# Last graph layer of a GNN kernel: where TensorE makes the relu inputs and the messages, relative to its table picks

## Reference

```python
h = relu(x @ pre_w1 + pre_b1) @ pre_w2 + pre_b2          # 16 -> 256 -> 256
msg = relu(h[src] @ conv_w + conv_b)                     # one row of 256 per edge
agg = segment_sum(msg, dst, num_segments=h.shape[0])
h = concatenate([h, agg], axis=-1)
out = tanh(relu(h @ post_w1 + post_b1) @ post_w2 + post_b2)
```

## Time and profile before

| | |
|---|---|
| median of 3 runs | 23847.17 us (23841.38 to 23860.08) |
| profiled execution | time 23829.4 us, span 23827.7 us |
| PE, matmuls | 19018.8 us busy, 80% of the span |
| DVE | 13388.2 us, 56% |
| POOL | 17485.7 us, 73% |
| ACT | 2359.5 us, 10% |
| `message_sums` | about 20054 to 23420 us of the span |

### The profile page before, as it was taken

The page is one execution under the profiler, slowest core; times in us unless marked ns, Lnnn a source line. Parts: engine busy times, 40 slices in busy tenths (PEclk is TensorE's granted clock), DMA queues, the critical chain, the costliest instruction groups (busy, mean ns, idle before and its releaser), DMA issues. The chain is left out here.

```text
span 23827.7 us, 301790 instructions
## 1 busy us (share of the span) xinstructions
PE 19018.8 (80%) x104646; PEld 12073.6 (51%) x104646; DVE 13388.2 (56%) x24950; ACT 2359.5 (10%) x5692; POOL 17485.7 (73%) x15117
## 2 busy tenths in 40 slices
PE   0688871787873488888888888499999988999997
PEld 0344431344442355555555555277777765555556
DVE  2688882454543366555555566355555543666662
ACT  0000000000000011111111111011111111111111
POOL 5777775777775788888888887588888853777775
PEclk9888885888886688888888888689999988999998
DMA  2222221111111112221111111133333313777773
GB/s 95 50 60 61 61 58 20 39 44 39 44 39 26 25 31 35 38 33 31 31 31 31 31 31 28 42 52 49 49 52 49 50 24 123 231 229 230 231 231 115
DMA packets 1967855, 1652.07 MB, mean 69 GB/s; under 512 B 781607, under 2 KB 1735622, under 8 KB 1949334
## 3 DMA queue, kind: packets, MB, share of 16 engines
q0 software_dynamic: 892288, 467.38, 14.2%
q10 hardware_dynamic: 821300, 579.22, 7.8%
q1 hardware_dynamic: 252898, 587.74, 7.3%
HBM read 949.01 MB, written 684.18 MB: 69 GB/s over the span
## 5 line engine op out<-in xcount | busy, mean ns | idle before, releaser
L1347 PE MATMUL node_sums<-placed_row,lane_values 128*128 128x392 bf16 x34500 | 6168.6, 338 | 524.6 <-DVE placed_row L1335 524.5
L1405 POOL DMA_INDIRECT acc<-column_sums,sum_rows x3375 | 5683.0, 1684 | 1192.8 <-issue 1139.8
L803 POOL DMA_INDIRECT gathered<-gat_table,src_index x4906 | 4853.9, 989 | 1525.2 <-issue 1500.3
L1347 PEld LDWEIGHTS node_sums<-placed_row,lane_values 128*128 128x128 bf16 x34500 | 3456.9, 102 | 2953.9 <-DVE placed_row L1335 548.7
L1626 POOL DMA_INDIRECT gathered<-sheaf_table,src_index x3125 | 3391.1, 1085 | 959.1 <-issue 946.5
L2408 POOL DMA_INDIRECT gathered<-message_table,src_index x2381 | 2428.6, 1020 | 907.9 <-issue 700.7
L1335 DVE TENSOR_SCALAR placed_row<-iota_rows_f,src_row 128x1568 bf16<-128x1568 f16 x2875 | 1794.5, 649 | 1116.3 <-PE node_sums L1347 1087.1
L1010 PE MATMUL lanes_ps<-S,table_parts 128*128 128x512 bf16 x8892 | 2075.7, 396 | 288.4 <-DVE S L875 288.4
L1010 PE MATMUL lanes_ps<-code_onehot,table_parts 128*128 128x512 bf16 x8892 | 2071.3, 396 | 276.1 <-DVE code_onehot L875 275.9
L1010 PEld LDWEIGHTS lanes_ps<-S,table_parts 128*128 128x128 bf16 x8892 | 896.0, 102 | 1411.0 <-DVE S L875 272.6
L2500 PE MATMUL lanes_ps<-code_onehot,table_parts 128*128 128x384 bf16 x9672 | 1597.9, 327 | 10.2 <-DVE code_onehot L2434 10.2
(11 more groups left out here) (478 smaller groups left out, 22582.7 us busy)
## 6 DMA issues: line engine op xcount, KB each, us to landing
message_rows<-gathered ACTq DMA_DIRECT2D x250, 1600.0 KB, 10.5
src_rows<-src_rows SPq DMA_DIRECT2D x200, 640.0 KB
src_rows<-src_rows SPq DMA_DIRECT2D x125, 960.0 KB
code_rows<-src_code_rows SPq DMA_DIRECT2D x336, 256.0 KB, 3.3
gat_rows<-scanned ACTq DMA_DIRECT2D x25, 3375.0 KB
gathered<-gat_table,src_index POOLq DMA_INDIRECT x4906
acc<-column_sums,sum_rows POOLq DMA_INDIRECT x3375
gat_rows<-scanned ACTq DMA_DIRECT2D x25, 2125.0 KB, 6.9
```

What stands on the lines that cost most here:

```text
L803: g.indirect_dma_start(G[b][:, j, :], None, tab, bass.IndirectOffsetOnAxis(ap=IX[b][:, j:j + 1], axis=0)).then_inc(s_g[b], 16)
L1347: last = pe.matmul(o.acc[:, m, 0:Q8 // 4], lane, o.OW[r][:, m * (Q8 // 4):(m + 1) * (Q8 // 4)], start=first(k, 1) and i == 0 and part == 0 ...
L1405: g.indirect_dma_start(self.acc[i], bass.IndirectOffsetOnAxis(ap=o.IXS[b][:, j:j + 1], axis=0), o.SV[b][:, j, :], None, compute_op=ALU.add ...
```

## The change

PE's steps for a set are written in another order, and ACT's with them. `hidden` (step 4) and `messages` (step 6) are now functions with a half as an argument. PE makes the relu inputs of half 0 after the first 21 of half 1's 39 picks (`FIRST` is 7, and 7 codes by 3 parts are 21). It makes the messages of half 1 after the first 21 picks of half 0 of the next set. The messages of half 0 and then the relu inputs of half 1 follow the picks. ACT copies half 1 of the set before at the start of its turn, and then does relus 0, copy 0, relus 1 and the DMAs. What is computed, and in how many instructions, stays the same; DVE's, POOL's and SP's programs are untouched in this function.

```diff
+                    def hidden(k, h):
+                        pe.wait_ge(s_mk, k * 2 + (h + 1))
+                        if not first(k, 1) or h == 1:
+                            pe.wait_ge(s_re, k * 2 + h)
+                        for m in range(2):
+                            last = pe.matmul(hp[m][:, 0:HE], W1R[:, m * P:(m + 1) * P], MK[h][:], start=True, stop=True)
+                        last.then_inc(s_hid, 1)
+
+                    def messages(k, h):
+                        pe.wait_ge(s_re, k * 2 + (h + 1))
+                        if not first(k, 1):
+                            pe.wait_ge(s_ev, k * 2 + (h - 1))
+                        for j in range(HB):
+                            to = op[h][j // 2][:, j % 2 * HID:(j % 2 + 1) * HID]
+                            for m in range(2):
+                                pe.matmul(to, HS[h][:, m, j * P:(j + 1) * P], WC[:, m, :], start=m == 0, stop=False)
+                            last = pe.matmul(to, ones[:], brow[:], start=False, stop=True)
+                        last.then_inc(s_out, 1)
+
                     def pick(k, b):
                         for h in range(2):
                             if not first(k, 1):
                                 pe.wait_ge(s_mk, k * 2 + (h - 1))
                             for t_ in range(CODES):
                                 if h == 0 and t_ in (0, FIRST):
+                                    if t_ and not first(k, 1):
+                                        messages(k - 1, 1)
                                     pe.wait_ge(s_og, k * 2 + (1 if t_ == 0 else 2))
+                                if h == 1 and t_ == FIRST:
+                                    hidden(k, 0)
                                 for i in range(PARTS):
...
-                        for h in range(2):
-                            pe.wait_ge(s_mk, k * 2 + (h + 1))
...
-                            last.then_inc(s_out, 1)
+                        messages(k, 0)
+                        hidden(k, 1)
                     chunks(pe, count - 1, peel, pick, RING)
+                    messages(count - 2, 1)
...
+                        if not first(k, 1):
+                            copy(k - 1, b, 1)
                         if not last_k(k):
-                            for h in range(2):
...
+                            relu(0)
+                            if not first(k, RING - 1):
+                                a.wait_ge(s_o[nb], 32 * ((k + 1) // RING) if isinstance(k, int) else k * 8 + (8 - 8 * nb))
+                            elif k == RING - 2:
+                                a.wait_ge(s_tb, 1)
+                            copy(k, nb, 0)
+                            relu(1)
                         a.wait_ge(s_done, k + 1)
```

More of the change, by code:

```diff
@@ L2533, in store @@
                         nb = (b + 1) % RING
-                        if not last_k(k):
[L2535 to L2551, removed]
@@ new lines, in relu, with copy @@
+                        def relu(h):
+                            a.wait_ge(s_hid, k * 2 + (h + 1))
+                            if not first(k, 1):
+                                a.wait_ge(s_out, k * 2 + (h - 1))
+                            for m in range(2):
+                                ins = nc.scalar.activation(HS[h][:, m, :], hp[m][:, 0:HE], ACT.Relu, bias=b1["pre_b1"][:, m:m + 1])
+                            ins.then_inc(s_re, 1)
+                        def copy(n, to, h):
+                            a.wait_ge(s_out, n * 2 + (h + 1))
+                            col = PC + h * HB
+                            nc.scalar.activation(G[to][:, col:col + 2, :], op[h][0][:].rearrange("p (a f) -> p a f", f=HID), ACT.Relu)
+                            nc.scalar.activation(G[to][:, col + 2, :], op[h][1][:, 0:HID], ACT.Relu).then_inc(s_ev, 1)
@@ new lines, in store @@
+                        if not first(k, 1):
+                            copy(k - 1, b, 1)
+                        if not last_k(k):
+                            relu(0)
[5 more added lines that the diff above has]
+                            relu(1)
```

## The result

The changed kernel takes 23897.57 us (median of 19 runs, 23861.49 to 23915.14), the kernel before 23849.57 us in the same measurement (19 runs). The ratio is 1.0019, with a 95% interval from 1.0012 to 1.0026: 48 us slower, between 29 and 62. The forecast was 36 us slower. A second measurement of the same kernel on another occasion gave 1.0016 (1.0007 to 1.0026).

What follows compares the result with a forecast made beforehand. It took PE, or a chain through it, as the bound. 121 sets x 0.36 = 43.6 us, less 3.9, 1.9 and 1.5 at the ends, gave +36 us on the median 23,847.17: 23,883 us, range 23,835 to 23,930.

Steps and rivals of the forecast that it cites:

- The wait of 1.31 us goes: PE's wait for ACT's relus before relu inputs of half 1 vanishes; a set 1.47 us shorter if nothing waited.
- A wait comes in its place, 27.18 us a set: PE waits 1.83 us for DVE's mask before relu inputs of half 0; closed chain 0.36 us over 26.82.
- The rule weighed in the prediction: PE's matmuls stay in program order, so the 18 picks don't fill the gap before relu inputs of half 0.
- What ACT gains or loses: nothing: ACT's copy of half 1 isn't held up by the second output DMA: 0 us, some 3 us of cover.
- The ends of the stage: First set 3.9 us shorter by an earlier clock rise, first interval 1.9 shorter, last set 1.5 shorter.
- Switching costs: PE's changes between bf16 picks and fp32 work, six a set for two: taken as 0, at most +44 us; 16%.
- The faster rival: Mask comes before PE asks, so PE bounds the set at 25.35 us: 23,660 us; 10%.
- the one-hots' cover: DVE's first seven one-hots end 0.44 us before the next set's picks; rival of their coming late +0 to +40, 7%.
- The clock as a rival: PE's clock falls in the new 1.67 us gap: +180 us, 24,065, possibly ten times that; 7%.

Runs made afterwards that it cites:

- mask13: The changed kernel with DVE's mask of half 0 behind 13 running sums in place of 12: 23983.28 us, ratio 1.0065 to the kernel before.
- mask14: The changed kernel with DVE's mask of half 0 behind 14 running sums in place of 12: 24108.71 us, ratio 1.0122 to the kernel before.
- mask8: The changed kernel with DVE's mask of half 0 behind 8 running sums in place of 12: 23786.02 us, ratio 0.9983 to the kernel before.
- g_messages_t3: The changed kernel with messages of half 1 after 9 of the next set's picks in place of 21: 23633.23 us, ratio 0.9918 to the kernel before.
- d2_messages_split: The changed kernel with the relu inputs of half 0 behind all picks, as in the kernel before: 24046.9 us, ratio 1.0094 to the kernel before.
- d_messages_only: The kernel before with only the messages of half 1 moved, after 21 picks of the next set: 24219.01 us, ratio 1.0164.

## Why the prediction was right

**The wait of 1.31 us goes.** Right: it is in no set of the changed kernel.

**A wait comes in its place, 27.18 us a set.** Right, at 27.20. The gap was forecast at 1.67 us and is 1.65; from the mask to the relu inputs it is 0.66 us as taken from the first set. That this chain is the cause is shown from three sides: it stretches by 0.55 and 1.06 us for one and two sums of 0.52 (mask13, mask14), the wait vanishes when the mask is earlier (mask8), and it vanishes when the whole chain starts earlier (g_messages_t3). The rule weighed in the prediction is borne out: the picks behind the gap don't fill it.

**What ACT gains or loses: nothing.** Right. The copy of half 1 starts at 21517.70, 0.11 us after the messages end, and the second output DMA had let go of the queue 3.2 us before (21510.19 + 4.31).

**The ends of the stage.** Right in kind, and a little small: the first set gives 5.6 us in place of 3.9, since the clock rose 1.4 us into the picks and not 4.6. The next interval is 1.9 shorter, as forecast, and the last 1.7 for 1.5. The 121 intervals between give 48 us for 43.6: a set is 0.38 longer and not 0.36, and one fall of the clock adds 1.7. Together the stage is 39 us longer, for 36 forecast; the two misses, 4 us more in the sets and 2 less at the ends, partly cancel.

**Switching costs.** The term of 0 that was taken is right; the fastest kernel has all six changes and PE's own work of 25.3 us.

**The faster rival was wrongly priced.** It said that without the wait for the mask PE would be the bound at 25.35 us. In the changed kernel's order it isn't: mask8 took that wait away and gained 0.7 us of the 1.8, since the one-hots bind next. I had both chains and had put the one-hots' cover at 0.44 us, but hadn't asked what they allow once the mask is early: 27.20 less the cover is 26.8, not 25.35, and 26.49 was measured.

**The clock as a rival** was right to be there. In the changed kernel's order the falls come at 2.2 us and more between records, and hardly at 1.65. But the length of the gap, by which the prediction judged it, isn't the whole: in another order 41 falls came behind gaps of 1.22 us (d2_messages_split).

**Which part did it.** The change has three moves: relu inputs 0 earlier, messages 1 later, and relu inputs 1 behind messages 0. The first alone makes the kernel faster (0.9965). The second alone does not leave it as it was: PE then waits for the mask of half 1, 28.01 us a set with the clock up. With the third it costs nothing where the clock stays up, but the clock falls in a third of the sets (1.0094). For the wait of the changed kernel, the one for the mask of half 0, it takes the first two together. Moving messages 1 behind 21 picks starts the chain that much later, moving relu inputs 0 ahead of 18 picks asks for its end that much earlier, and the chain needs 8.17 us from the end of messages 1. Either move alone leaves 57 or 60 picks (9.3 or 9.8 us) of the 78 as cover; both leave 39 (6.34 us).

The median of the whole run moved by 48 us and the stage by 39. The 39 lie within the interval of the 48 (29 to 62); whether the 9 us between them have a cause stays open.

## What to carry to other kernels

When work is moved to hide a wait, follow the longest chain that runs through a third engine, and count how much work the moving engine has between the chain's start and the point where it needs the chain's end; two moves that each leave enough of that cover can together take too much, since they take it from both sides (here 60 and 57 picks alone, 39 together, of 78). Each move alone has to be followed through the other waits too, as messages 1 alone showed. Then ask the same of the next chain, and put the start of the chains as early as the wait that the move was to hide allows: here 9 picks were worth 1% against 21. An experiment that removes a wait is also the quickest way to see which one is next.

## What the runs showed of the hardware that was not expected

- The clock fell behind shorter gaps than feared, and the length of the gap alone doesn't tell when. It fell 41 times in 122 gaps of 1.22 us with messages behind them (d2_messages_split), and never in 122 gaps of 1.31 us in the kernel before, where the relu inputs of half 1 stand behind them. With relu inputs and then picks behind the gap it fell once in two profiles at 1.65 us (244 gaps), 30 times in 122 at 2.2 and 67 times at 2.7. With relu inputs and then messages behind it, it fell 74 times in 122 at 2.6 (d_messages_only).
- What a fall costs differs from run to run and within one. With picks close behind it lasts 3.4 us and a set is 1.7 us longer (mask13, mask14). In d2_messages_split it lasts 10.2 us and costs 4.8. In d_messages_only it lasts 3.4 us in 49 sets, ending amid the messages, and 13.7 us in 25. In the kernel before, the messages of the first set ran at half clock throughout, some 18 us with PE busy. The Trainium skill ("TensorE: Matmul & The Clock Gate", Part 1) says that the clock is held low by default and that activity releases it. The record agrees in that all 212 falls of the four runs named ended with PE at work, 163 amid picks and 49 amid messages; but messages ended them in some sets and not in others, and what decides this stays open.
- 0.80 us in place of 0.39 between DVE's last sum and its one-hots, in every fourth set, where DVE's loop over four sets turns.
